# A transformer block on 64 small images: the last stage reordered with joint small passes, two bank assignments, the load order and two queue orders changed

## The reference, cut to what matters

```python
def tok(img):                                   # patches: (64, 36, 768)
    x = layernorm(x, ln1_g, ln1_b)
    x = x @ W + bias
    x = layernorm(x, ln2_g, ln2_b) + pe[None]
    return concatenate((cls_token + cls_pos_embedding, x), axis=1)   # (64, 37, 256)

def attn(x):                                    # 16 heads of 16
    q, k, v = split(x @ Wqkv + bqkv)
    q = q * cos + rotate_half(q) * sin          # k alike
    probs = softmax(q @ k.T / sqrt(16))
    return (probs @ v) @ Wout + bout

def bitlinear(x, W, b):                         # ternary weights, 8-bit tokens
    w_scale = clip(mean(abs(W)), EPS)
    Wq = clip(round(W / w_scale), -1, 1) * w_scale
    x_scale = clip(max(abs(x), axis=-1), EPS)
    xq = round(x * (127 / x_scale)) * (x_scale / 127)
    return xq @ Wq.T + b

h = tok(x)
h = h + attn(layernorm(h))
h = h + bitlinear(gelu(bitlinear(layernorm(h), W1, b1)), W2, b2)     # 256 -> 1024 -> 256
```

## Time and profile before

| what | us |
|---|---|
| time before, median of 3 runs | 336.23 |
| its runs | 335.48, 336.23, 338.11 |
| the profiled execution's own time | 335.01 |
| its span in the profile | 333.2 |
| busy PE / DVE / ACT / POOL | 304.5 / 254.3 / 195.0 / 138.9 |
| start and patch stage, roughly | 0 to 155 |
| attention, roughly | 155 to 238 |
| last stage | 238 to 333.2 |

### The profile page before, as it was taken

One profiled execution on the slowest core, in us unless ns is written; L12 is line 12 of the kernel. 1 busy time (PEld: TensorE's weight loads), 2 busy tenths in 40 slices (PEclk: granted clock), 3 DMA queues, 4 the chain that ended last, 5 costly groups with the idle time before them and its releaser, 6 DMA issues.

```text
span 333.2 us, 9403 instructions
## 1 busy us (share of the span) xinstructions
PE 304.5 (91%) x3575; PEld 232.7 (70%) x3583; DVE 254.3 (76%) x666; ACT 195.0 (59%) x366; POOL 138.9 (42%) x262
## 2 busy tenths in 40 slices
PE   8989899999999977998999999999768999999784
PEld 8877676777777644656877777877645777776552
DVE  1778996677757774356888877887489999999982
ACT  0323433545544335447655666655548999999992
POOL 0356665645654467437900000000065565666520
PEclk9999999999999999999999999999999999999996
DMA  6799560010000100113211121111000001000011
GB/s 227 230 369 401 165 223 17 18 36 17 19 17 17 36 17 17 51 35 79 54 42 44 40 47 45 40 47 29 3 0 0 3 32 34 31 33 31 33 48 55
DMA packets 19307, 22.38 MB, mean 67 GB/s; under 512 B 2304, under 2 KB 15888, under 8 KB 19264
## 3 DMA queue, kind: packets, MB, share of 16 engines
q1 hardware_dynamic: 18544, 20.89, 19.3%
q10 hardware_dynamic: 720, 0.90, 1.0%
HBM read 16.76 MB, written 5.02 MB: 65 GB/s over the span
## 4 chain that ended last, share of the span: by engine, by line
PE 68%; DVE 18%; ACT 8%; issue 4%; POOL 1%; DVEq 0%; ACTq 0%
PE ps L414 15%; PE ps L454 10%; PE ps L528 9%; DVE sc L913 7%; PE ps L551 7%; PE ps L432 5%; DVE ximg L934 4%; PE ps L518 4%; PE ps L402 4%; PE ps L536 3%; ACT ximg L1125 3%; PE ps L462 2%; ACT ximg L1120 2%; PE ps L499 2%; PE ps L393 2%
## 5 line engine op out<-in xcount | busy, mean ns | idle before, releaser
L1159 POOL TENSOR_TENSOR rs<-rs,nhalf 128x1 f32<-128x1 f32 (+1 forms) x76 | 45.4, 597 | 159.2 <-DVE rs L907 101.2
L414 PE MATMUL ps<-w_in,xT 128*128 128x256 f32 (+1 forms) x228 | 52.6, 380 | 0.6 <-ACT xT L992 0.6
L414 PEld LDWEIGHTS ps<-w_in,xT 128*128 128x128 f32 (+1 forms) x228 | 41.2, 187 | 6.5 <-ACT xT L992 0.8
L1077 ACT ACTIVATE ximg<-ps 128x296 f32<-128x296 f32 x64 | 26.6, 418 | 30.0 <-PE ps L528 29.4
L998 ACT ACTIVATE hn<-h,nmr,rs 128x256 f32<-128x256 f32 (+1 forms) x19 | 11.4, 600 | 54.9 <-POOL nmr L1179 54.9
L454 PE MATMUL ps<-w_qk,hnT 128*128 128x512 f32 (+1 forms) x76 | 36.2, 598 | 3.5 <-DVE qb L793 3.5
L528 PE MATMUL ps<-tab,ximg 128*128 128x128 f32 x256 | 34.9, 279 | 0.0
L851 DVE TENSOR_REDUCE ximg<-ps 128x16 f32<-128x592 f32 x32 | 24.7, 772 | 13.3 <-PE ps L518 13.1
L1166 POOL TENSOR_TENSOR qa<-qa,qb 128x512 f32<-128x512 f32 (+1 forms) x19 | 24.1, 1266 | 13.0 <-DVE qb L793 13.0
L528 PEld LDWEIGHTS ps<-tab,ximg 128*128 128x128 f32 x256 | 27.4, 141 | 1.3
L714 DVE SCALAR_TENSOR_TENSOR h<-ymid,rs,ps 128x256 f32<-128x256 f32 (+1 forms) x19 | 9.1, 480 | 24.8 <-PE ps L393 20.4
(11 more groups left out here) (110 smaller groups left out, 666.6 us busy)
## 6 DMA issues: line engine op xcount, KB each, us to landing
ximg<-in_x SPq DMA_DIRECT2D x18, 384.0 KB, 10.3
ximg<-vsc SPq DMA_DIRECT2D x64, 51.0 KB, 1.9
vsc<-vt SPq DMA_DIRECT2D x18, 136.0 KB, 1.7
out<-ximg SPq DMA_DIRECT2D x18, 128.0 KB, 1.7
ximg<-in_W SPq DMA_DIRECT2D x2, 1024.0 KB, 6.3
qkT<-in_W SPq DMA_DIRECT2D x2, 384.0 KB, 4.8
wide<-in_rows SPq DMA_DIRECT2D x1, 640.0 KB, 10.5
qkT<-in_offsets ACTq DMA_DIRECT2D x1, 512.0 KB, 4.0
```

Source lines behind the costliest of these rows:

```text
L414: mm = pe.matmul(dst[0:n, :], xT[t % 2][:, k, 0:n], w_in[:, k, :], start=(k == 0), stop=(k == KP - 1))
L1077: act.activation(pT[p % 2][:, g0:g0 + 4, :, :], ps_pT(b), ACT.Copy).then_inc(S[f"p_evac{b}"], 1)
L1159: pool.tensor_tensor(rs[u][0:n, i:i + 1], rs[u][0:n, i:i + 1], nhalf[0:n, :], ALU.pow).then_inc(S[done], 1)
```

## The change

- *Last stage.* The two small passes on DVE (`step_size`, `steps_per_unit`), one pair for the tokens and one for the hidden rows of a tile, become one pair that works on two columns at once: those of token tile `j` and of hidden tile `j-3` (`step_sizes`, `steps_per_unit`). `rescale` on POOL becomes one instruction as well. `token_var` moves from DVE to POOL, `tokens_rounded` from ACT to POOL. ACT's order becomes gelu, hidden_rounded, hidden_out, n_out. On PE `turn_hidden` and `down` run one step later than before (tiles `s-6` and `s-8`), and `turn_n` ahead of `down`.
- *Between attention and last stage.* `out_product` of tiles 0 to 2 is placed between the last attention steps on PE. On DVE `residual(0)`, `(1)` and `(2)` stand ahead of `normalise` of the pairs 29, 30 and 31. The wait for the ternary weights (`w_done`) moves behind these. ACT loads the table for gelu ahead of the copies of the last two pairs.
- *Queries.* `qk_product` of tiles 11, 13 and 15 goes to bank 1 (free once the last pixels are copied), 17 to bank 4, and from tile 11 on it waits for the rotation of the tile two before. `scores(0)` waits for the rotation of tile 15.
- *Pixels.* On ACT `pixels_out(s)` is the first operation of steps 3 to 8, where it was the last.
- *Start.* 9 products of ones instead of 13; SP waits for the first half of W before it issues pixel tile 0.

```diff
         def qk_bank(t):
-            return 4 if t > NT - LAG + 2 and t % 2 else 6
+            if t % 2 == 0 or t <= NT - LAG + 1:
+                return 6
+            return 4 if t == NT - 1 else 1
...
             sp.dma_start(w_raw[:, 3:6, :], w_rows[:, 3:6, :]).then_inc(S["ld_w1"], 16)
+            sp.wait_ge(S["ld_w0"], 16)
             load_x(0)
...
             def qk_product(t):
                 pe.wait_ge(S["h_canvas"], t + 1)
-                war(pe, "qk_rot", t, 2 if t > NT - LAG + 3 else 1)
+                war(pe, "qk_rot", t, 2 if t > NT - LAG + 1 else 1)
...
+                if qk_bank(t) == 1:
+                    pe.wait_ge(S["x_evac"], NT + 1)
...
-            for i in range(13):
+            for i in range(9):
...
+            pe.wait_ge(S["qk_rot"], NT - 2)
             scores(0)
...
-            attention_step(NP + 1)
-            ffn_step(0)
-            attention_step(NP + 2)
-            for s in range(1, NT + 8):
+            pe.wait_ge(S["s_sub"], NP)
+            out_product(0)
+            turn_out(NP - 3)
+            attend(NP - 2)
+            turn_probs(NP - 1, 4)
+            turn_probs(NP - 1, 5)
+            out_product(1)
+            turn_out(NP - 2)
+            attend(NP - 1)
+            out_product(2)
+            turn_out(NP - 1)
+            pe.wait_ge(S["w_done"], 2)
+            for s in range(3, NT + 9):
                 ffn_step(s)
...
+            def step_sizes(j):
+                if j <= NT:
+                    v.wait_ge(S["r_amax"], j + 1)
+                if j >= 3:
+                    v.wait_ge(S["f_amax"], j - 2)
+                v.tensor_scalar(sc[j % 8][:, 2:4], sc[j % 8][:, 0:2], EPS, 1.0 / QB, ALU.max, ALU.mult
+                                ).then_inc(S["q_xs"], 1)
...
+            residual(0)
+            normalise(NP - 3)
+            token_stats(0)
+            token_mean(0)
+            residual(1)
+            normalise(NP - 2)
+            token_stats(1)
+            token_mean(1)
+            largest("r", 0, hn[0], 0, 0, "r_norm")
+            step_sizes(0)
+            residual(2)
+            steps_per_unit(0)
+            normalise(NP - 1)
...
             def patch_step(s):
+                if s < LAG:
+                    pixels_out(s)
...
-                if live(s, NT + 1):
+                if live(s, NT + 1) and s >= LAG:
                     pixels_out(s)
...
+            def tokens_rounded(t):
+                pool.wait_ge(S["q_rc"], t + 1)
+                n = rows(t)
+                pool.tensor_scalar(hn[t % 2][0:n, :], hn[t % 2][0:n, :], sc[t % 8][0:n, 4:5], MAGIC,
+                                   ALU.mult, ALU.add).then_inc(S["r_rnd"], 1)
...
             def ffn_step(s):
                 if live(s, NT + 1):
+                    token_var(s)
                     inverse_root(3, s, s % 2, "r_var", "r_rstd")
                     token_shift(s)
                 if live(s - 1, NT + 1):
+                    tokens_rounded(s - 1)
+                if live(s - 2, NT + 1):
+                    add_down_offset(s - 2)
+                if live(s, NT + 1):
+                    tokens_normal(s)
+                if live(s - 1, NT + 4):
+                    rescale(s - 1)
```

More of the change, by code:

```diff
@@ L654, in _ @@
             v.memset(ones_c[:, :], 1.0)
+            v.memset(steps_of[:, :, :], 1.0)
             v.memset(less_magic[:, :], -MAGIC)
@@ L884, in _ @@
             v.memset(ps[:, 7, 0:NH * VW], 1.0).then_inc(S["a_init"], 1)
-            for s in range(3, NP + 3):
+            for s in range(3, NP):
                 attention_step(s)
@@ L902, in token_mean, with largest, steps_per_unit @@
                 v.bn_aggr(mv[t % 2][0:n, 3, :], st[t % 2][0:n, 0, :]).then_inc(S["r_aggr"], 1)
[L904 to L910, removed]
+            def largest(x, c, src, t, j, before):
                 v.wait_ge(S[before], t + 1)
                 n = rows(t)
-                v.tensor_reduce(sc[t % 8][0:n, c:c + 1], src[0:n, :], AX.X, ALU.max, apply_absolute_value=True
+                v.tensor_reduce(sc[j % 8][0:n, c:c + 1], src[0:n, :], AX.X, ALU.max, apply_absolute_value=True
                                 ).then_inc(S[f"{x}_amax"], 1)
[L916 to L925, removed]
+            def step_sizes(j):
[5 more added lines that the diff above has]
+                                ).then_inc(S["q_xs"], 1)
+            def steps_per_unit(j):
+                v.wait_ge(S["q_xs"], j + 1)
+                v.reciprocal(sc[j % 8][:, 4:6], sc[j % 8][:, 2:4]).then_inc(S["q_rc"], 1)
             def hidden_sum(t):
@@ L1096, in _ @@
             patch_step(NT + LAG + 2)
-            for s in range(2, NP + 3):
+            for s in range(2, NP + 1):
                 attention_step(s)
             act.preload_act_table(ACT.Gelu)
+            attended_out(NP - 2)
+            attended_out(NP - 1)
             act.wait_ge(S["m_set"], 1)
-            def tokens_rounded(t):
-                act.wait_ge(S["r_rc"], t + 1)
-                n = rows(t)
-                act.activation(hn[t % 2][0:n, :], hn[t % 2][0:n, :], ACT.Identity, bias=magic[0:n, :],
-                               scale=sc[t % 8][0:n, 2:3]).then_inc(S["r_rnd"], 1)
             def n_out(t):
@@ L1135, in ffn_step @@
             def ffn_step(s):
+                if live(s - 2, NT + 1):
+                    gelu(s - 2)
                 if live(s - 3, NT + 1):
                     hidden_rounded(s - 3)
-                if live(s - 2, NT + 1):
-                    gelu(s - 2)
-                if live(s - 1, NT + 1):
-                    n_out(s - 1)
+                if live(s - 4, NT + 1):
+                    hidden_out(s - 4)
                 if live(s, NT + 1):
-                    tokens_rounded(s)
-                if live(s - 3, NT + 1):
-                    hidden_out(s - 3)
-            for s in range(NT + 4):
+                    n_out(s)
+            for s in range(NT + 5):
                 ffn_step(s)
```

78 lines of the change are left out of this document (34 added, 44 removed).

## The result

| | median us | runs | ratio to before |
|---|---|---|---|
| before, all its runs | 335.86 | 335.27 to 338.11 | |
| changed kernel | 327.29 | 326.29 to 328.25 | 0.973, 95% interval 0.970 to 0.976 |

The changed kernel is 8.6 us (2.7%) faster. Its profiled execution took 328.25 us, span 326.4; between the two profiled executions the gain is only 6.8 us, since the one of before lies 0.85 us under its median and the one of the changed kernel, the slowest of its four, 0.96 above its own.

A forecast was written before the change was run, and what follows sets the result against it. Each stage has its own limit: DVE paces the last stage, PE the patch steps once all products run. Gains of 4.6 + 1.8 + 0.45 + 0.6 = 7.5 us against 336.23 gave 328.7 us, range 324.5 to 334.0.

The forecast's parts named there:

- The step in mid stage: Last stage, hidden sum to hidden sum: DVE sets the pace and sheds 0.24 us a step, 4.17 to 3.93 us.
- Early steps: First steps of the last stage, which have no `finish` yet: 3.64 us a step.
- The transition: Between attention and last stage: PE and DVE take turns, so the first hidden sum comes 1.4 us later.
- Rival B: Transition hidden: PE and DVE find other work, the last stage starts 2 to 4 us earlier; 324 us; 12%.
- Behind the last hidden sum: End of the last stage: the last reciprocal now follows a `finish`, about +0.2 us.
- Last stage in all: The last stage, transition included, ends 4.6 us earlier.
- Pixels first: Early patch steps: PE no longer waits for pixel copies; 1.8 us gained, bounds 0.5 and 3.
- Queries in bank 1: Last patches: two rotation waits go, copies of turned queries are late next; 0.45 us gained, upper bound 3.5.
- Start: Start of the program: 4 fewer products of ones; 0.6 us gained, bounds 1.8 gain and 1 loss.
- A: Last stage: DVE's 128x2 step size pass waits for POOL's root; 7.6 us come back, 336.3, no change; 15%.
- C: Transition and first last-stage steps: TensorE falls to 1.2 GHz, costing 11 us; 339.7 us; 3%.
- D: Last stage: PE is the limit at 4.1 us a step; stage gain only 2.5, total 330.8 us; 20%.

The follow-up runs named there:

- e6: The changed kernel with the last stage's variance pass back on DVE instead of POOL; 327.82 us.
- e8: The changed kernel with each joint 128x2 pass of DVE (step size, reciprocal) split into two 128x1 passes; 328.99 us.
- e5: The changed kernel with each normalise ahead of its residual on DVE again in the transition, PE's order kept; 324.01 us.
- e4: The changed kernel with the pixel, query and start edits all undone, leaving the last stage with its transition; 329.84 us.
- e1: The changed kernel with ACT copying a tile's pixels at the end of each early patch step again; 329.05 us.
- e2: The changed kernel with late odd queries in banks 6 and 4 again, old waits, no rotation wait ahead of scores(0); 327.99 us.
- e3: The changed kernel with the old start: 13 products of ones and no SP wait for the first half of W; 328.26 us.
- e9: The changed kernel with one extra, unused DVE pass over 128x256 floats (even, odd or two-input) in each last-stage step; 331.06 us, one run.
- e11: Run e5 with the joint step size pass of the last stage moved from DVE to POOL; 323.32 us.
- e7: The changed kernel with ACT rounding the tokens again, behind gelu, instead of POOL; 329.28 us.

## Why the prediction was right

Forecast 328.7 us (324.5 to 334.0), measured 327.29: the result lies in the range and the forecast's case came true. Its terms one by one:

- *The step in mid stage*, forecast 3.93, is 3.89. Of the 0.28 saved, 0.06 is the variance (e6) and 0.11 the two separate passes (e8). Half of the other 0.11 is the old order, in which one step size pass cost 0.12 (275.48 to 275.60 in the earlier trace rows) where now it costs 0.07 (281.69 to 281.76); the rest is hundredths on the larger passes. (The prediction's sum goes on from 3.93 with 3.95 a step.) To price from start to start, not by duration, was the right step: by durations the three passes would have been 0.41.
- *Early steps* 3.64 forecast, 3.63 measured; *at the end* 3.56 forecast, 3.52 to 3.66 measured.
- *The transition*, forecast 1.4 longer, is 0.65 longer. The mechanism stood (e5); its size was taken 0.75 too high. The turns of residual and normalise took 3.4 as forecast (233.79 to 234.90 and so on), the three products 3.6 instead of 3.8, and PE's remaining attention work, my estimate of 3.8, took 3.2. Rival B (12%) had the transition hidden; e5 shows that this was to be had, but in another order.
- *Behind the last hidden sum*, +0.2 forecast, +0.6 measured. From the last wide maximum to the last rounding on ACT it is 318.24 - 316.23 = 2.0 us instead of 1.6, because a `finish` stands ahead of the reciprocal; 0.2 more lies on PE, where `turn_hidden` now stands behind a `down`. The prediction took the first at half its size and missed the second.
- *Last stage in all*: forecast 4.6, in the traces 0.65 + 0.6 - 6.7, that is 5.4 gained; e4, in which only this part is left, gained 5.8 against before.
- *Pixels first*: 1.8 forecast, 1.46 in the trace of e1 and 1.8 in its time. The product is at 50.05 instead of 52.58, and it starts just as the copy that it waits for ends, as the prediction had it.
- *Queries in bank 1*: 0.45 forecast, 0.20 measured in e2's trace. The two waits, 1.85 and 1.69 us there, were mostly covered, as the working said. It took what is left from the copies of turned queries, at twice its size; the 0.2 is there already at the last copy of turned h, 62.43 us behind that of tile 8 instead of 62.62.
- *Start*: 0.6 forecast, 1.0 by e3's time and 0.96 between the profiles. The weight means start 1.70 us earlier (5.04 instead of 6.74) and last 0.74 longer (3.67 instead of 2.93) in the profiled pair. This term was too small, since it charged the real products more than that; in four of the nine traces they took 2.75 us, no longer than behind 13 products of ones.

Sum of the terms as now measured: 5.4 + 1.65 + 0.96 = 8.0 us, against 7.5 forecast and 8.6 between the medians. That the forecast came this close is in part luck: the last stage was taken 0.8 and the start 0.4 too low, pixels and queries together 0.6 too high. The profiled pair shows 6.8 because of the attention, 1.25 us longer in unchanged code. From the last query copy to the last softmax, all thirteen traces of the changed kernel and its variants lie from 0.2 to 2.25 us above the one trace of before, spread over 2.0 us; PE's gaps there are partly put down to nothing the profile shows. Whether that is scatter or, say, where the code lies, wasn't tried and stays open.

Rivals. A: no row of mid stage shows the 128x2 pass held; e9 shows that its mechanism works at 128x256, where the change puts no such pass. B: false for the change, true for e5. C: the clock was granted in full in the transition and in the whole last stage, at 2.4 GHz. D: the busy shares can't decide it, since in mid stage PE has hardly a gap either (43.47 us busy of 44 from 260 to 304). The experiments do: the step follows what is put on DVE (3.95 in e6, 4.00 in e8) and what is taken off it (3.82 in e11), so PE's work is 3.82 a step at most.

## What to carry to other kernels

On an engine without gaps, price a small instruction by the distance between two starts; here that is 0.06 us where its record says 0.15, and it held for adding as for removing one. Where two engines take turns, ask which of the two waiting operations already has its data and put that one first: swapping two operations on DVE, in three places, gave 3.4 us here, more than any other single edit in these experiments. Work moved off an engine that isn't the limit in mid stage can still pay at the stage's ends, where the limit changes (e7).

## What the runs showed of the hardware

- Executions differ in when the first products reach full speed: 12 passes from about 5.0 us on took from 2.75 to 3.67 us in the same code, with the granted clock at 1.00 (2.4 GHz) in all these rows. One trace can't price an edit at the start to better than 1 us.
- DVE and POOL do hold each other up on 128x256 SBUF passes (e9). The one whose recorded start comes second isn't always the one that waits: with DVE 0.10 to 0.11 us behind, POOL's 0.48 us became 0.64 or 0.78; with DVE 0.14 behind and POOL idle before, DVE's 0.27 became 0.48.
- ACT's instructions overlap as well: 4.63 us of durations fit into 3.93 us without a gap, some 0.14 each (e7).
